# Token transposes of an attention group: four in one step, or spread over three, with the centring on another engine

## The chip, the cores and the metric

One Trainium2 chip, one of its cores. The metric is the device time of the whole program in microseconds (us); the kernel is launched once. TensorE multiplies matrices, VectorE, ScalarE and GpSimd work on tiles of 128 rows, and SyncE (SP) issues the DMAs. In the profile they are PE (with PEld for its weight loads), DVE, ACT, POOL and SP.

## The reference

`x` is 64 graphs of 128 tokens with 512 features, `adj` a 128 x 128 mask for each graph. Two passes of masked attention with 8 heads of 64 features run one after the other, then a feed-forward layer. What is computed, cut to what matters:

```python
def attention_side(source, query_source, mask):        # n2e, then e2n
    q, k, v = query_source @ wq.T + bq, source @ wk.T + bk, source @ wv.T + bv
    w = softmax(where(mask > 0, q_h @ k_h.T * 64 ** -0.5, -inf))   # 8 heads
    return concat(w @ v_h)
edges = ln(attention_side(x, x, adj.T) + x, norm1_g, norm1_b)
nodes = ln(x + attention_side(edges, x, adj), norm2_g, norm2_b)
out = ln(nodes + gelu(nodes @ w1.T + b1) @ w2.T + b2, norm3_g, norm3_b)
return layernorm(x + out)
```

`ln(y)` is `(y - mean) / sqrt(var + eps) * g + b` over the 512 features of a token. The change lies between the mean and variance of the first two of these norms and the transposed result that the next pass reads.

## The kernel before, in words

The 8192 tokens are worked off in 16 groups of 4 graphs (512 tokens), once for each attention pass, so there are 32 attention groups g = 0 to 31 (0 to 15 the first pass, 16 to 31 the second), and then 16 groups of the feed-forward pass. Every fp32 operand of a projection is split in a high and a low part, and three matmuls make one product.

**A group is four steps**, u = 0 to 3, one for each pair of heads. On TensorE a step is: keys of the pair (12 matmuls of 128 x 512), queries (12), `weigh` (the probabilities of an earlier step times the values, 40 small matmuls into `att_out`), values of one graph (12), then `scores` of this step (12 matmuls of 128 x 256). `weigh` lags two steps: step u of group g weighs pair u - 2, and steps 0 and 1 weigh pairs 2 and 3 of the group before. So the tokens of group g - 1 are complete only in step 1 of group g. Values run ahead by two steps too: steps 0 and 1 make the values of graphs 2 and 3 of the group, steps 2 and 3 those of graphs 0 and 1 of the next.

**The other engines in a step.** VectorE: for the scores of the step before, mask and maximum (8 instructions, `mask_and_maximum`, L763), `value_rest` (L739), the low part of the probabilities (L772), the low parts of keys and queries (L744, L747, L752), and then `add_weighed` (L688 to L710), which adds the residual and takes the statistics; in step 1 it ends with the group's mean and variance (`att_moments`). ScalarE: 8 exponentials (L525), the high parts of probabilities, keys and queries, then splits of the source or of the queries, and the value's high part (L508). GpSimd: `value_low` (L631, L633) for each graph, the low part of the source, and the bias of the residual (`add_bias`, L651).

**The norm of group g - 1** runs beside group g. GpSimd's `inverse_spread` stands behind `value_low` of graph 3, which is in step 2: it waits for the moments, then makes var + eps (L614), minus the mean (L615), the inverse square root as a power (`att_rstd`, L617) and the product `att_offset` (L620). ScalarE's `centre` (L486) then applies scale and offset to the four graphs, in step 2 behind the queries' high part. The result stands in `att_even_sum` or, in odd groups, in `normed`. In step 3 come the **token transposes**: `turn` (L838) puts one graph's 128 x 512 as four 128 x 128 blocks through TensorE into the one bank `att_turn`, and ScalarE's `copy_turned` (L478, four instructions) applies gain and shift on the way to one of the two buffers of `turned`, from which SyncE's `store_turned` writes to DRAM. There is one bank, so a `turn` waits until the copy before it is done:

```python
turn 0; keys; turn 1; queries; weigh; turn 2; values; turn 3; scores     # step 3 on TensorE
```

**The order of the work** is written out by hand for each engine; there is no scheduler. Semaphores count upward (`centred`, `turned_ready`, `turned_copied`). SyncE's queue is in order as well: a `store_turned` that waits for its copy holds the loads and probability transposes behind it. The groups of a pass run as two written out, six rounds of a loop of two groups, and two written out (`over_groups`), so each engine jumps back five times in a pass; a group that begins behind such a jump is called a jump group here, the other groups plain.

## Time and profile before

| | |
|---|---|
| median of 3 runs | 3041.64 us (3040.52 to 3041.72) |
| the profiled execution, its own time | 3036.6 us |
| its span, first to last instruction | 3034.8 us |
| busy: PE, DVE, ACT, POOL | 2895.0, 1618.3, 1633.8, 1297.0 us |
| mean granted TensorE clock | 0.992 |

The page shows TensorE busy in nine tenths of nearly every slice. The two attention passes take about the first 1573 us, the feed-forward pass the rest. Busy time of TensorE says little alone, since its matmuls overlap each other; its idle time is read from the waits and from the timeline, which name what ended each wait.

### The profile page before, as it was taken

Reading aid. Unit: us, or ns where it says so; the run is one execution under the profiler, and the core shown is the slowest. Engines: PE = TensorE matmul, PEld = TensorE weight load, DVE = VectorE, ACT = ScalarE, POOL = GpSimd, SP = SyncE. Lnnn points to the kernel's source line nnn. Section 1 sums busy time; section 2 is a strip of 40 time slices with the busy share of each in tenths; the row PEclk is TensorE's granted clock in tenths of the full one; section 3 lists DMA queues with packets and bytes.
Section 4 is the critical chain, followed back from the end, with each engine's and each line's share of the span. In section 5 each row is a group of like instructions: output and inputs, shape, how many; then the busy total and the mean of one; then the engine's idle time right before and its main releaser. Section 6 shows DMA issues by size and latency. Waiting matters only on the chain.

```text
span 3034.8 us, 55254 instructions
## 1 busy us (share of the span) xinstructions
PE 2895.0 (95%) x17920; PEld 2397.2 (79%) x17920; DVE 1618.3 (53%) x5786; ACT 1633.8 (54%) x4266; POOL 1297.0 (43%) x1291
## 2 busy tenths in 40 slices
PE   8999999999899999999989999999999999999996
PEld 7888878788787777787867888888888888888885
DVE  7776877777776767676763323232332323233234
ACT  6778777778788887888874222222222222222221
POOL 3443534344355555555431443444344344434434
PEclk9999999999999999999999999999999999999998
DMA  6554544454566565656563011111011111100101
GB/s 192 119 117 119 116 113 111 110 124 118 131 161 157 149 163 143 167 142 163 139 171 118 29 56 49 56 55 55 28 35 55 48 55 55 55 28 34 56 35 63
DMA packets 488660, 295.40 MB, mean 97 GB/s; under 512 B 279585, under 2 KB 410785, under 8 KB 488481
## 3 DMA queue, kind: packets, MB, share of 16 engines
q1 hardware_dynamic: 488480, 293.49, 36.2%
q8 instruction: 53, 0.87, 0.1%
q14 instruction: 127, 1.03, 0.1%
HBM read 159.21 MB, written 67.11 MB: 75 GB/s over the span
## 4 chain that ended last, share of the span: by engine, by line
PE 58%; issue 21%; POOL 14%; ACT 3%; DVE 2%; DMA 1%; POOLq 0%; SPq 0%; ACTq 0%; DVEq 0%
PE proj L1336 23%; PE score L1350 12%; PE proj L1350 11%; PE proj L872 9%; POOL att_tokens L651 4%; POOL att_v L633 3%; POOL source_lo L646 3%; PE score L919 2%; POOL att_v L631 2%; POOL att_query_lo L640 1%; PE att_out L856 1%; ACT att_probs L525 1%; ACT turned L478 1%; POOL pool_scratch L101 1%; POOL att_rstd L617 1%
## 5 line engine op out<-in xcount | busy, mean ns | idle before, releaser
L1122 ACT ACTIVATE hidden<-proj,ffn_bias 128x512 f32<-128x512 f32 x256 | 176.4, 689 | 1016.5 <-PE proj L1336 1016.5
L1282 DVE TENSOR_TENSOR hidden_lo<-hidden,hidden_hi 128x512 fp32r<-128x512 f32 x256 | 203.6, 795 | 966.2 <-ACT hidden_hi L1115 966.2
L525 ACT ACTIVATE att_probs<-att_probs,att_minus_max 128x128 f32<-128x128 f32 x1024 | 397.2, 395 | 115.5 <-DVE att_minus_max L763 115.5
L101 POOL TENSOR_TENSOR pool_scratch<-pool_scratch 128x1 f32<-128x1 f32 x144 | 41.4, 288 | 731.2 <-DVE ffn_moments L1226 415.2
L772 DVE TENSOR_TENSOR att_p_lo<-att_probs,att_p_hi 128x512 f16<-128x512 f32 x256 | 188.5, 776 | 292.0 <-ACT att_p_hi L532 292.0
L763 DVE CUSTOM_DVE_ANT_0 att_probs<-score,att_mask 128x128 f32<-128x128 f32 x1024 | 226.3, 285 | 29.2 <-issue 15.6
L646 POOL TENSOR_TENSOR source_lo<-source_raw,source_hi 128x512 fp32r<-128x512 f32 x128 | 163.0, 1295 | 152.0 <-ACT source_hi L548 152.0
L478 ACT ACTIVATE turned<-att_turn,att_shift,att_gain 128x128 f32<-128x128 f32 x512 | 193.2, 459 | 63.6 <-PE att_turn L838 62.2
L872 PE MATMUL proj<-weight_v_hi,source_hi 128*128 128x512 f32 x512 | 211.9, 414 | 13.6 <-DVE weight_v_lo L722 11.1
L872 PE MATMUL proj<-source_hi,weight_k_hi 128*128 128x512 f32 x512 | 203.4, 397 | 3.7 <-DVE weight_k_lo L722 3.7
L1336 PE MATMUL proj<-source_hi,w_hi 128*128 128x512 f32 x512 | 201.7, 394 | 0.0
L1336 PE MATMUL proj<-source_lo,w_hi 128*128 128x512 f32 x512 | 201.7, 394 | 0.0
L1336 PE MATMUL proj<-source_hi,w_lo 128*128 128x512 f32 x512 | 201.7, 394 | 0.0
L872 PE MATMUL proj<-weight_v_hi,source_lo 128*128 128x512 f32 x512 | 201.6, 394 | 0.0
L525 ACT ACTIVATION_READ_ACCUMULATOR att_probs<-att_probs,att_minus_max 128x1 f32 x1024 | 197.6, 193 | 6.4 <-issue 6.4
L872 PE MATMUL proj<-source_hi,weight_k_lo 128*128 128x512 f32 x512 | 201.1, 393 | 0.0
L872 PE MATMUL proj<-source_lo,weight_k_hi 128*128 128x512 f32 x512 | 200.8, 392 | 0.0
L872 PE MATMUL proj<-weight_v_lo,source_hi 128*128 128x512 f32 x512 | 200.7, 392 | 0.0
L856 PEld LDWEIGHTS att_out<-att_v,att_pt_hi 128*128 128x128 f16 x3072 | 149.1, 98 | 37.8 <-issue 37.8
L1213 POOL TENSOR_TENSOR normed<-normed,gain_row 128x512 f32<-128x512 f32 x64 | 83.9, 1311 | 211.6 <-DMA normed<-nodes 211.6
L651 POOL TENSOR_TENSOR att_tokens<-att_tokens,bias_row 128x512 f32<-128x512 f32 x128 | 167.9, 1312 | 1.7 <-DMA att_tokens<-in_x 1.7
L919 PE MATMUL score<-att_k_hi,att_q_hi 128*128 128x256 f32 x512 | 148.6, 290 | 18.9 <-DVE att_q_lo L752 18.9
(159 smaller groups left out, 8550.3 us busy)
## 6 DMA issues: line engine op xcount, KB each, us to landing
att_tokens<-in_x SPq DMA_DIRECT2D x128, 256.0 KB, 3.0
source_raw<-in_x_t SPq DMA_DIRECT2D x16, 1024.0 KB, 5.7
edges_t<-turned SPq DMA_DIRECT2D x64, 256.0 KB, 2.5
source_raw<-edges_t SPq DMA_DIRECT2D x16, 1024.0 KB, 5.8
att_query_raw<-in_x_t SPq DMA_DIRECT2D x16, 1024.0 KB, 6.6
nodes_t<-turned SPq DMA_DIRECT2D x64, 256.0 KB, 2.6
source_raw<-nodes_t SPq DMA_DIRECT2D x16, 1024.0 KB, 7.9
normed<-nodes SPq DMA_DIRECT2D x16, 1024.0 KB, 5.7
```

The costliest lines, as they stand in the source:

```text
L478: last = nc.scalar.activation(turned[:, b % 2, c, :], turn_bank[:, c * P:(c + 1) * P], ACT.Identity, bias=shift_column[own][:, c:c + 1], s ...
L525: nc.scalar.activation(probs[:, j, :], probs[:, j, :], ACT.Exp, bias=minus_max[:, j:j + 1], scale=-1.0, accum_out=row_sum[:, side, j:j + 1 ...
L646: nc.gpsimd.tensor_tensor(source_lo[1 - parity][:, c, :], source_raw[:, c, :], source_hi[1 - parity][:, c, :].bitcast(F32), ALU.subtract). ...
L651: nc.gpsimd.tensor_tensor(pair(tokens, u), pair(tokens, u), bias_v[:, u * P:(u + 1) * P].rearrange("p (o d) -> p o d", o=1).to_broadcast([ ...
L763: nc.vector.tensor_tensor_reduce(out=probs[:, 4 * h + j, :], in0=score_bank[h][:, j * P:(j + 1) * P], in1=mask[:, 2 * h + j // 2, :], scal ...
L772: nc.vector.tensor_tensor(p_lo[:, 4 * h:4 * h + 4, :], probs[:, 4 * h:4 * h + 4, :], p_hi[:, 4 * h:4 * h + 4, :], ALU.subtract).then_inc(p ...
L856: last = nc.tensor.matmul(out, p, value, start=(i == 0), stop=(i == len(products) - 1))
L872: last = nc.tensor.matmul(bank[:], stationary, moving, start=(c == 0 and i == 0), stop=(c == C - 1 and i == 2))
L919: last = nc.tensor.matmul(score_bank[h][:, 2 * i * P:2 * (i + 1) * P].rearrange("p (s j) -> p s j", s=2), q, k, start=(n == 0), stop=(n == 2))
L1282: nc.vector.tensor_tensor(hidden_lo[:, c % 2, :], hidden[:, c % 2, :], hidden_hi[:, c % 2, :].bitcast(F32), ALU.subtract).then_inc(hidden_ ...
L1336: last = nc.tensor.matmul(up_bank[c % 2][:], w, s, start=(i == 0), stop=(i == len(products) - 1))
L1350: last = nc.tensor.matmul(down_bank[b][:], h, w, start=(c == 0 and i == 0), stop=(c == FC - 1 and i == 2))
```

## The change

Three things move; nothing is computed differently but for the form of the centring.

1. **TensorE.** For a group's norm, `turn` 0 now stands in step 2 of the next group, between queries and `weigh`; `turn` 1 in the same step in the middle of the values (`midway`); `turn` 2 in step 3 behind `weigh`; and `turn` 3 in step 0 of the group after that, behind `weigh`. In the last group (g = 31) turns 1 and 3 stand before the scores of steps 2 and 3.
2. **ScalarE** copies 0 and 1 at the end of step 2, copy 2 in step 3, copy 3 in step 0, and centres no more. **SyncE** stores graph 0 one place earlier and graph 3 behind a probability transpose in the next group's step 0.
3. **GpSimd** drops minus the mean and the offset, and centres itself right behind the inverse square root: four instructions `(y - mean) * rstd` on 128 x 512, then the queries' low parts and `add_bias` as before.

The diff, without the declarations:

```diff
@@ SyncE, the body of a group
             load_tokens(sp, g, own, 1)
-            if not below(g, 2):
-                store_turned(sp, g - 2, own, GB - 1)
...
             if not starts(g):
                 turn_probabilities(sp, C * g - 1)
+            if not below(g, 2):
+                store_turned(sp, g - 2, own, 3)
...
             turn_probabilities(sp, C * g + 1)
+            if not starts(g):
+                store_turned(sp, g - 1, before, 0)
...
             if not starts(g):
-                store_turned(sp, g - 1, before, 0)
                 store_turned(sp, g - 1, before, 1)
@@ ScalarE
-    def centre(act, g, parity, b):
-        if b == 0:
-            act.wait_ge(offset_ready, g + 1)
-        data = total[parity][:, b, :]
-        nc.scalar.activation(data, data, ACT.Identity, bias=offset[:, b:b + 1], scale=rstd[:, b:b + 1]).then_inc(centred, 1)
...
-                turning = u == C - 1 and not starts(g)
-                if turning:
-                    copy_turned(act, g - 1, before, 0)
...
                 key_high(g, own, u)
-                if turning:
-                    copy_turned(act, g - 1, before, 1)
                 query_high(g, own, u)
                 if u < 2:
                     split_source(g, parity, range(2 * u, 2 * u + 2))
+                if u == 0 and not below(g, 2):
+                    copy_turned(act, g - 2, own, 3)
                 if u == 2 and not starts(g):
-                    for b in range(GB):
-                        centre(act, g - 1, 1 - parity, b)
-                if turning:
+                    copy_turned(act, g - 1, before, 0)
+                    copy_turned(act, g - 1, before, 1)
+                if u == 3:
                     if own == 1 and after == 1:
                         split_queries(g + 1)
-                    copy_turned(act, g - 1, before, 2)
-                    copy_turned(act, g - 1, before, 3)
+                    if not starts(g):
+                        copy_turned(act, g - 1, before, 2)
+                    if at(g, last_group - 1):
+                        copy_turned(act, g - 1, before, 3)
@@ GpSimd
         nc.gpsimd.tensor_scalar(spread[:], moments[:, :, 1], EPS, None, ALU.add).then_inc(spread_ready, 1)
-        nc.gpsimd.tensor_scalar(minus_mean[:], moments[:, :, 0], -1.0, None, ALU.mult).then_inc(negated, 1)
         pool.wait_ge(spread_ready, g + 1)
         nc.gpsimd.tensor_tensor(rstd[:], spread[:], half[:], ALU.pow).then_inc(rstd_ready, 1)
-        pool.wait_ge(negated, g + 1)
-        pool.wait_ge(rstd_ready, g + 1)
-        nc.gpsimd.tensor_tensor(offset[:], minus_mean[:], rstd[:], ALU.mult).then_inc(offset_ready, 1)
+
+    def centre(pool, g, parity):
+        pool_gate(pool, rstd_ready, g + 1, pool_scratch)
+        for b in range(GB):
+            data = total[parity][:, b, :]
+            nc.gpsimd.tensor_scalar(data, data, moments[:, b, 0:1], rstd[:, b:b + 1], ALU.subtract, ALU.mult).then_inc(centred, 1)
...
             if not starts(g):
                 inverse_spread(pool, g - 1)
+                centre(pool, g - 1, 1 - parity)
@@ TensorE
+                if midway is not None and c == 1:
+                    turn(pe, *midway)
...
             for u in range(C):
-                turning = u == C - 1 and not starts(g)
-                if turning:
+                keys(g, parity, own, u)
+                queries(g, parity, own, u)
+                if u == 2 and not starts(g):
                     turn(pe, g - 1, 1 - parity, 0)
-                keys(g, parity, own, u)
-                if turning:
-                    turn(pe, g - 1, 1 - parity, 1)
-                queries(g, parity, own, u)
                 if u >= 2:
                     weigh(pe, g, parity, u - 2)
                 elif not starts(g):
                     weigh(pe, g - 1, 1 - parity, u + 2)
-                if turning:
+                if u == 0 and not below(g, 2):
+                    turn(pe, g - 2, parity, 3)
+                if u == 3 and not starts(g):
                     turn(pe, g - 1, 1 - parity, 2)
                 if u < 2:
                     values(g, parity, own, u + 2)
                 elif not at(g, last_group - 1):
-                    values(g + 1, 1 - parity, after, u - 2)
-                if turning:
-                    turn(pe, g - 1, 1 - parity, 3)
+                    values(g + 1, 1 - parity, after, u - 2, (g - 1, 1 - parity, 1) if u == 2 and not starts(g) else None)
+                if at(g, last_group - 1):
+                    if u == 2:
+                        turn(pe, g - 1, 1 - parity, 1)
+                    if u == 3:
+                        turn(pe, g - 1, 1 - parity, 3)
```

How instructions stand now. GpSimd before, in the second group of the loop, from `value_low` of graph 3 to the next bias (`pool_scratch` rows are one-column instructions that carry a wait inside the loop):

```order
L631 CAST att_v_1<-att_v_rest 128x512
L632 REGISTER_ALU
L633 TENSOR_TENSOR att_v_1<-att_v_rest,att_v_1 128x512 [waits att_v_middle_ready]
L101 TENSOR_TENSOR pool_scratch<-pool_scratch 128x1 [waits att_moments_ready]
L614 TENSOR_SCALAR att_spread<-att_moments 128x4
L615 TENSOR_SCALAR att_minus_mean<-att_moments 128x4
L617 TENSOR_TENSOR att_rstd<-att_spread,minus_half 128x4 [waits att_spread_ready]
L620 TENSOR_TENSOR att_offset<-att_minus_mean,att_rstd 128x4 [waits att_rstd_ready,att_negated]
L651 TENSOR_TENSOR att_tokens<-att_tokens,bias_row 128x4x128 [waits att_tokens_in3]
```

The same place of the changed kernel (its lines are numbered a few lower):

```order
L628 CAST att_v_1<-att_v_rest 128x512
L629 REGISTER_ALU
L630 TENSOR_TENSOR att_v_1<-att_v_rest,att_v_1 128x512 [waits att_v_middle_ready]
L101 TENSOR_TENSOR pool_scratch<-pool_scratch 128x1 [waits att_moments_ready]
L609 TENSOR_SCALAR att_spread<-att_moments 128x4
L611 TENSOR_TENSOR att_rstd<-att_spread,minus_half 128x4 [waits att_spread_ready]
L101 TENSOR_TENSOR pool_scratch<-pool_scratch 128x1 [waits att_rstd_ready]
L617 TENSOR_SCALAR att_even_sum<-att_even_sum,att_moments,att_rstd 128x512 x4
L648 TENSOR_TENSOR att_tokens<-att_tokens,bias_row 128x4x128 [waits att_tokens_in3]
```

The four centring instructions stand between the inverse square root and the bias, still behind `value_low` of graph 3. TensorE, the same loop, step 2 of the changed kernel, from the last query matmul to the scores (before, the row of `att_out` with its waits followed the queries directly, and no transposes stood in this step):

```order
L836 MATMUL att_turn<-att_identity,normed 128x128 [waits att_turned_copied,att_centred]
L836 MATMUL att_turn<-att_identity,normed 128x128 x3
L843 ISA
L845 ISA [waits att_summed,att_values_ready]
...
L877 ISA
...
L836 MATMUL att_turn<-att_identity,normed 128x128 [waits att_turned_copied,att_centred]
L836 MATMUL att_turn<-att_identity,normed 128x128 x3
```

The first transposes of a group now ask for the centring ahead of `weigh` of step 2, and the second stand between the two halves of the values.

## Rows read from the trace of the kernel before

**Rows 1.** The page, groups of instructions: busy us, mean ns | idle before, releaser.

```profile
L478 ACT ACTIVATE turned<-att_turn,att_shift,att_gain 128x128 f32<-128x128 f32 x512 | 193.2, 459 | 63.6 <-PE att_turn L838 62.2
```

**Rows 2.** Waits of TensorE over the whole span: waited for, us in total, times, longest.

```profile
PE att_turn L838 <- ACT turned L478: 62.2, 47, 3.4
```

**Rows 3.** Windows of four groups, from keys of step 0 to the next: length, busy (instructions), clock, DMA.

```profile
392.70:441.99 49.29, 46.03 (x371) 38.72 (x370) 37.05 (x163) 37.64 (x113) 20.62 (x25) 1.00 0.48 113
441.99:489.18 47.19, 45.62 (x370) 38.73 (x369) 34.63 (x152) 37.50 (x113) 20.38 (x25) 1.00 0.49 117
1129.47:1177.64 48.17, 45.91 (x371) 38.68 (x370) 34.81 (x152) 39.47 (x117) 26.38 (x30) 1.00 0.61 158
1177.64:1228.51 50.87, 46.28 (x370) 38.60 (x369) 35.91 (x163) 39.60 (x117) 25.47 (x30) 1.00 0.59 150
```

**Rows 4.** Timeline of TensorE, first pass: start us, us, engine, line, [idle before, releaser].

```profile
416.22 0.40 PE L872 MATMUL proj<-source_hi,weight_k_hi 128*128 128x512 f32 x1
...
422.14 0.25 PE L856 MATMUL att_out<-att_v,att_pt_hi 128*128 128x64 bf16 x3 [0.29 <-POOL att_v L633]
...
427.58 0.60 PE L838 MATMUL att_turn<-att_identity,normed 128*128 128x128 f32 x4
...
427.94 0.48 PE L872 MATMUL proj<-source_hi,weight_k_hi 128*128 128x512 f32 x1
...
463.84 0.40 PE L872 MATMUL proj<-source_hi,weight_k_hi 128*128 128x512 f32 x1
...
474.77 0.60 PE L838 MATMUL att_turn<-att_identity,att_even_sum 128*128 128x128 f32 x4
```

**Rows 5.** Timeline of VectorE, first pass: the first mask-and-maximum of a step.

```profile
394.74 0.29 DVE L763 CUSTOM_DVE_ANT_0 att_probs<-score,att_mask 128x128 f32<-128x128 f32 x1
...
406.30 0.28 DVE L763 CUSTOM_DVE_ANT_0 att_probs<-score,att_mask 128x128 f32<-128x128 f32 x1
...
417.45 0.28 DVE L763 CUSTOM_DVE_ANT_0 att_probs<-score,att_mask 128x128 f32<-128x128 f32 x1
...
441.46 0.29 DVE L763 CUSTOM_DVE_ANT_0 att_probs<-score,att_mask 128x128 f32<-128x128 f32 x1 [0.68 <-issue]
...
463.67 0.29 DVE L763 CUSTOM_DVE_ANT_0 att_probs<-score,att_mask 128x128 f32<-128x128 f32 x1
```

**Rows 6.** Timeline of GpSimd, step 2 of one group of the first pass.

```profile
420.05 0.61 POOL L631 CAST att_v<-att_v_rest 128x512 bf16<-128x512 f32 x1
...
420.74 1.17 POOL L633 TENSOR_TENSOR att_v<-att_v_rest,att_v 128x512 bf16<-128x512 f32 x1
...
422.57 0.57 POOL L614 TENSOR_SCALAR att_spread<-att_moments 128x4 f32<-128x4 f32 x1
...
423.42 1.04 POOL L617 TENSOR_TENSOR att_rstd<-att_spread,minus_half 128x4 f32<-128x4 f32 x1
...
424.60 0.20 POOL L620 TENSOR_TENSOR att_offset<-att_minus_mean,att_rstd 128x4 f32<-128x4 f32 x1
...
424.75 1.29 POOL L651 TENSOR_TENSOR att_tokens<-att_tokens,bias_row 128x512 f32<-128x512 f32 x1
```

**Rows 7.** Timeline of ScalarE in the same step: the centring.

```profile
424.83 2.93 ACT L486 ACTIVATE normed<-normed,att_offset,att_rstd 128x512 f32<-128x512 f32 x4 [0.82 <-POOL att_offset L620]
```

**Rows 8.** Timeline of VectorE, second pass: the first mask-and-maximum of steps 0 and 2.

```profile
1178.72 0.29 DVE L763 CUSTOM_DVE_ANT_0 att_probs<-score,att_mask 128x128 f32<-128x128 f32 x1
...
1203.15 0.28 DVE L763 CUSTOM_DVE_ANT_0 att_probs<-score,att_mask 128x128 f32<-128x128 f32 x1
```

**Rows 9.** Timeline of ScalarE, second pass, behind the loop's jump: a gap between exponentials.

```profile
1184.30 0.20 ACT L525 ACTIVATION_READ_ACCUMULATOR att_probs<-att_probs,att_minus_max 128x1 f32 x1 [1.37 <-issue]
```

**Rows 10.** Timeline of TensorE: the third transposes of group 31.

```profile
1565.97 0.63 PE L838 MATMUL att_turn<-att_identity,att_even_sum 128*128 128x128 f32 x4 [3.45 <-ACT turned L478]
```

**Rows 11.** Timeline of TensorE: the keys behind its longest wait between the passes.

```profile
782.58 0.79 PE L872 MATMUL proj<-source_hi,weight_k_hi 128*128 128x512 f32 x1 [3.69 <-DVE weight_k_lo L722]
```

**Rows 12.** Windows: those twelve key matmuls, columns as in rows 3.

```profile
782.58:787.03 4.45, 4.45 (x12) 3.23 (x12) 3.71 (x7) 3.05 (x7) 0.00 (x0) 0.65 0.00 2
```

18 lines of the change are left out of this document (7 added, 11 removed).

## The prediction

> **What bounds the kernel now.** I read the page first, where TensorE is busy nearly throughout and ScalarE's copies idle mostly for TensorE [rows 1], then TensorE's waits, then windows and timelines of single groups. Of TensorE's waits the largest in the attention passes is the one that the change aims at: transposes wait 62.2 us in 47 places for the copy that empties their bank [rows 2]. The windows [rows 3] show what a group takes, from the keys of step 0 to those of the next group: in the first pass 49.29 us behind the loop's jump and 47.19 in a plain group, in the second 50.87 and 48.17. Nothing is slowed there by TensorE's clock, granted in full in all four. A step without transposes takes TensorE 10.93 us (463.84 to 474.77, rows 4), a block of four transposes 0.36 us (427.58 to 427.94, rows 4). Four steps and four blocks are 45.2 us, so 2 to 5.7 us of a group are waits.
>
> TensorE is not alone at the limit. VectorE's step, from one first mask-and-maximum to the next, takes 11.15 us in step 1 (406.30 to 417.45, rows 5), more than TensorE's 10.93. What stands in step 2 behind VectorE and GpSimd is therefore late by nature: GpSimd's cast of the values starts only at 420.05 [rows 6], and `weigh`, with everything else done, waits 0.29 us for GpSimd at 422.14 [rows 4]. The new place of the first transposes is in front of that `weigh`, and they wait for more of GpSimd than it does.
>
> **The change, part by part.** *Removed.* The 62.2 us of waits for the copy [rows 2] go. The copies have time now: between blocks 0 and 1 TensorE does `weigh` and half the values, some 2.6 us, and a copy takes 1.5 (193.2 us over 128 copies, rows 1) and two hand-overs; the other gaps are whole steps. ScalarE loses 2.93 us of centring in each group [rows 7]. I cost that at nothing: it lay beside TensorE's values and scores.
>
> *The new wait: when the first transposes can start.* I count from M, the first mask-and-maximum of step 2 (417.45, rows 5). From there GpSimd gets the last value, and its chain is shown [rows 6]. The variance instruction ends at 423.14; with a hand-over of 0.14 (424.46 to 424.60) the power starts at 423.28, 0.14 earlier than now, since minus the mean is gone, and ends at 424.32. The one-column instruction with its wait and the hand-over behind it are 0.14 each, so centring starts at 424.60. Then one centring, then 0.23 to reach TensorE (421.91, the end of the value's subtraction, to `weigh` at 422.14).
>
> No row shows a GpSimd instruction with two scalars per row on 128 x 512. The nearest below is the cast of one tensor, 0.61 us, the nearest above the addition of two tensors, 1.29 us [rows 6]. It reads one tensor, so I stay by the cast and take 0.70 for the second operation. The transposes then start at 425.53, that is M + 8.08.
>
> The Trainium skill (GPSIMD Engine Reference, Elementwise — side-by-side cycle accounting) gives 2.6 cycles an element for two inputs and 769 ns as the measured best case for 512 elements of a tight loop; by that the sum would be 2 us higher. The same page (Engine selection) speaks against moving elementwise work to GpSimd at all; here it is not the duration but the place in the chain that costs.
>
> *What follows them.* Block 0.36, `weigh` to the end of scores 5.44 (422.14 to 427.58, rows 4), block 1 0.36, then step 3 with block 2, 11.29: together 17.45 us to the next group's keys.
>
> *Plain group.* Counted from its keys at 441.99 [rows 3]: the first mask stands at -0.53 (441.46, rows 5), bound by the scores. Step 0 carries block 3 now, 11.29, so the next mask is at 10.76; 11.15 later, at 21.91, comes M. Transposes at 29.99, next keys at 47.44. TensorE would have been there after 11.29 + 10.93 + 5.6 (keys and queries, 416.22 to the end before 422.14), at 27.8: it waits 2.2 us. Against 47.19 that is +0.25 in the first pass, against 48.17 it is -0.73 in the second [rows 3].
>
> *Jump group.* VectorE's first mask comes 2.04 late (394.74 against 392.70), M 22.71 behind it [rows 5]: transposes at 32.83, TensorE there at 29.1, a wait of 3.7 us; the group takes 50.28 against 49.29, +0.99. In the second pass M comes 24.43 behind the first mask [rows 8], 1.37 of it a gap in ScalarE's exponentials that waits for nothing shown [rows 9]. If the gap stays, 52.00 against 50.87, +1.1; if it goes (ScalarE jumps earlier now), -0.2. I take the middle, +0.45.
>
> *Sum.* Nine plain and five jump groups in each pass: 9 x 0.25 + 5 x 0.99 - 9 x 0.73 + 5 x 0.45 = +2.9. At the ends of the passes, group 31 waits 3.45 us for a copy [rows 10] and group 15 the average of 1.3 (62.2 over 47); about 1 us is left where two blocks stand around one `weigh`: -4. Without the clock: -1.1.
>
> *The clock.* Behind an idle time of 3.69 us [rows 11] twelve key matmuls took 4.45 us at a mean granted clock of 0.65 [rows 12], that is for a part at 1.2 GHz instead of 2.4, where twelve otherwise take 2.8: 1.65 lost. The four windows, with waits of 1.3 us on average, hold the full clock [rows 2, 3]; in the ten jump groups there would be one of 3.7 us each. I take four falls, +6.6; the bounds are none, 0, and all ten, +16.5.
>
> The Trainium skill (TensorE: Matmul & The Clock Gate, HAM oscillation) warns of just this pattern, a wait in every round that lets the clock fall in every round. By it the sum would take all ten, 10 us more.
>
> Edits with one answer: the stores move behind copies that move too. The store of graph 0 stands in front of a token load that must wait for step 2's sums anyway, the store of graph 3 in front of one that waits for step 0's; the next use of each buffer is a step away. GpSimd's four centrings, 2.8 us, delay only the bias behind them, 1.29 us [rows 6], whose sums are read a step later, and the next value; GpSimd is busy 21 to 26 us of a group [rows 3], so there is room. In the feed-forward pass they stand alone.
>
> So +5.5 on the profiled execution's own 3036.6 us: 3042.1. The median of the three runs lies 5.0 above that execution: **3047 us**.
>
> **The rivals.**
>
> *A slow centring on GpSimd (slower).* At 1.29 us, like the addition, every group's transposes wait 0.59 more: 31 x 0.59 = 18.3, and waits of 4.3 us in jump groups let the clock fall in eight, +6.6: 3072. Each tenth costs 3.1 us; from 0.75 on the result is more than 0.2% above. For it: two operations and two scalars. Against it: the cast's time.
>
> *The clock holds and the gap goes (faster).* Centring at 0.61 (-2.8), no fall (-6.6), ScalarE's gap gone (-3.4): 3034. For it: ScalarE is two microseconds freer at the jump, and the waits of now cost no clock in the windows. Against it: 3.69 us did.
>
> *The wait is simply gone (faster).* If the first transposes didn't wait at their new place, all 62.2 us would go: 2979. It needs a chain 3.7 us shorter in the jump groups and 2.2 in the plain ones; nothing in rows 6 leaves that, but a place where the order differs from what I see can't be excluded.
>
> *SyncE's queue (slower).* A store that waits for its copy holds the transposes of probabilities behind it. At 1 us a group: 3078. It decides only if a copy comes over 4 us later than I have it.
>
> **How the numbers follow.** A measurement of this kernel tells about 0.2%, 6 us, from no change. Forecast 0.46: its own bounds (centring 0.61 to 0.85, clock falls 0 to 10) run from 3038 to 3061, so faster 0.04, within 0.22, slower 0.20. Slow centring 0.20, all slower. Clock and gap 0.24: 0.18 faster, 0.06 within. Wait gone 0.04. Queue 0.06. Faster 0.26, within 0.28, slower 0.46. The range 3026 to 3074 leaves out the wait that is gone, the queue and the tails.
>
> **What would show it.** In TensorE's waits the row of transposes waiting for the copy nearly vanishes, and one of transposes waiting for GpSimd's centring takes its place, with 70 to 80 us, 2.2 in plain groups and 3.7 in jump groups. The centring's mean time is 0.7. The second pass's plain groups take 47.4 us. The granted clock drops in some jump groups of step 2. I am wrong if the first transposes start well before M + 8, if the waits are gone without a new one, or if plain groups of both passes fall below 46.5.

## The result, and the profile after

The changed kernel takes 3089.99 us (median of 4 runs, 3087.70 to 3092.62), the kernel before on the same chip 3041.08 us (4 runs). The ratio is 1.0162, with a 95% interval of 1.0144 to 1.0180: slower by 1.6%, outside the noise. The profiled execution has a span of 3090.8 us against 3034.8, +56.0, and that difference is what the following takes apart.

The page of the change, TensorE's busy time first, then the group that answers to [rows 1] (columns as there):

```profile
PE 2909.6 (94%) x17920; PEld 2437.4 (79%) x17920; DVE 1658.5 (54%) x5786; ACT 1548.6 (50%) x4138; POOL 1564.1 (51%) x1379
...
L480 ACT ACTIVATE turned<-att_turn,att_shift,att_gain 128x128 f32<-128x128 f32 x512 | 192.5, 457 | 205.9 <-PE att_turn L836 205.8
```

The copies take as long as before, and idle three times as long for the transposes, which costs nothing: they have time now. TensorE's waits, the view of [rows 2]:

```profile
PE att_turn L836 <- POOL normed L617: 63.9, 15, 4.8
...
PE att_turn L836 <- POOL att_even_sum L617: 52.5, 16, 3.7
...
PE score L919 <- DVE att_q_lo L750: 10.1, 11, 1.5
...
PE att_turn L836 <- ACT turned L480: 2.6, 2, 2.1
```

The wait for the copy has gone from 62.2 to 2.6 us, as meant. In its place stand 116.4 us of waits for GpSimd's centring, one in each of 31 groups: 4.8 us in the jump groups, 2.6 to 3.8 in the others. (The third row, the waits of the scores for VectorE's low part of the queries, was 18.9 us before.) Where the waits for the centring come from shows on GpSimd in step 2 of a group behind the loop's jump, the stretch that answers to [rows 6]:

```profile
447.45 0.61 POOL L628 CAST att_v<-att_v_rest 128x512 bf16<-128x512 f32 x1
...
448.14 1.17 POOL L630 TENSOR_TENSOR att_v<-att_v_rest,att_v 128x512 bf16<-128x512 f32 x1
...
449.88 0.67 POOL L609 TENSOR_SCALAR att_spread<-att_moments 128x4 f32<-128x4 f32 x1
...
450.64 1.03 POOL L611 TENSOR_TENSOR att_rstd<-att_spread,minus_half 128x4 f32<-128x4 f32 x1
...
451.93 4.14 POOL L617 TENSOR_SCALAR normed<-normed,att_moments,att_rstd 128x512 f32<-128x512 f32 x2
```

The last row is two of the four centrings, 4.14 us, so 2.07 each; the means over the span are 2.09 and 2.13. The chain up to it is as in [rows 6]. TensorE gets its first block in a plain group and in this one at:

```profile
402.05 0.66 PE L836 MATMUL att_turn<-att_identity,att_even_sum 128*128 128x128 f32 x4 [3.29 <-POOL att_even_sum L617]
...
454.06 1.12 PE L836 MATMUL att_turn<-att_identity,normed 128*128 128x128 f32 x4 [4.82 <-POOL normed L617]
```

The second of these rows has more to tell than its 4.82 us of wait. Its four transposes take 1.12 us instead of 0.66. From the transposes to the end of the scores the same 72 matmuls ran in both groups. Their windows, columns as in [rows 3], and behind them the window of the attention passes as a whole:

```profile
402.05:408.43 6.38, 6.38 (x72) 5.80 (x73) 3.01 (x18) 3.66 (x10) 6.38 (x4) 1.00 0.50 102
...
454.06:462.53 8.47, 8.46 (x72) 7.67 (x73) 3.10 (x18) 3.66 (x10) 7.38 (x4) 0.73 0.48 96
...
50.00:1690.00 1640.00, 1497.88 (x11644) 1268.15 (x11643) 1181.83 (x4883) 1143.46 (x3475) 975.61 (x890) 0.96 0.52 129
```

Behind the wait of 3.29 us the clock was at 1.00, behind that of 4.82 us at 0.73 on average, that is for about half of the stretch at 1.2 GHz instead of 2.4, and the stretch took 2.1 us more. Over the attention passes the mean clock is 0.96. Before it was 0.99:

```profile
50.00:1610.00 1560.00, 1458.67 (x11635) 1227.30 (x11635) 1138.35 (x4877) 1225.43 (x3597) 714.22 (x805) 0.99 0.55 135
```

In the trace's record of the granted clock the change has 27 stretches at half clock before the span's last one, 133 us in all; such a stretch is called a fall here. They follow the first transposes in all ten jump groups and in 13 of the other 21, and four stand at the ends of the passes. The kernel before has 3, 24 us, all at the ends of the passes. What a fall costs can be read from plain groups of the change that differ in nothing else, from the keys of step 0 to the next: without a fall, with one of 3.4 us, with one of 6.8 us:

```profile
370.89:419.74 48.85, 45.56 (x370) 38.74 (x369) 36.87 (x156) 34.96 (x108) 28.92 (x28) 1.00 0.46 113
...
473.84:524.25 50.41, 47.12 (x370) 39.93 (x369) 36.84 (x154) 34.97 (x108) 28.92 (x28) 0.97 0.45 110
...
578.91:630.29 51.38, 48.09 (x371) 40.94 (x370) 36.81 (x154) 34.97 (x108) 28.92 (x28) 0.93 0.44 108
```

That is 1.6 us for the shorter and 2.5 us for the longer.

**A part that the change does not touch became faster.** I divide the span at one instruction that is the same in both, the first matmul of the feed-forward pass with weights in a tile named `w..._hi`. It stands before and after at

```profile
1617.03 0.39 PE L1350 MATMUL score<-w_hi,hidden_hi 128*128 128x512 f32 x1
```

```profile
1695.63 0.39 PE L1346 MATMUL score<-w_hi,hidden_hi 128*128 128x512 f32 x1
```

So the part up to it grew by 78.6 us, and the rest, 1417.8 us before, is 1395.2 us, 22.6 less. The two parts are called attention and feed-forward below, though the first holds some 44 us of the feed-forward pass's beginning as well. In the same 300 us of full clock and full load TensorE ran 1304 matmuls before and 1325 after (windows of before, then of after):

```profile
2000.00:2300.00 300.00, 300.00 (x1304) 244.22 (x1303) 91.23 (x178) 78.75 (x123) 123.51 (x104) 1.00 0.16 54
```

```profile
2000.00:2300.00 300.00, 300.00 (x1325) 248.43 (x1324) 90.53 (x175) 78.36 (x122) 118.83 (x98) 1.00 0.16 54
```

### The profile page after: what moved, and what is told of

It is laid out like the page before. It is cut to its first block, busy times and chain, and to the rows that moved or that the text cites. A ratio compares the mean times of both kernels' runs of the same rounds, so it can differ in the third digit from the quotient of the medians.

```text
span 3090.8 us, 55194 instructions
## 1 busy us (share of the span) xinstructions
PE 2909.6 (94%) x17920; PEld 2437.4 (79%) x17920; DVE 1658.5 (54%) x5786; ACT 1548.6 (50%) x4138; POOL 1564.1 (51%) x1379
## 3 DMA queue, kind: packets, MB, share of 16 engines
q1 hardware_dynamic: 488480, 293.49, 35.5%
## 4 chain that ended last, share of the span: by engine, by line
PE 53%; POOL 23%; issue 18%; DVE 3%; ACT 1%; DMA 1%; POOLq 0%; SPq 0%; DVEq 0%; ACTq 0%
PE proj L1332 22%; PE score L1346 11%; PE proj L1346 11%; PE proj L870 6%; POOL att_tokens L648 4%; POOL normed L617 3%; POOL att_even_sum L617 3%; POOL source_lo L643 3%; POOL att_v L630 3%; POOL att_v L628 2%; POOL att_query_lo L637 1%; POOL pool_scratch L101 1%; PE att_out L854 1%; POOL att_rstd L611 1%; PE score L919 1%
## 5 line engine op out<-in xcount | busy, mean ns | idle before, releaser
L101 POOL TENSOR_TENSOR pool_scratch<-pool_scratch 128x1 f32<-128x1 f32 x168 | 47.7, 284 | 673.5 <-DVE ffn_moments L1222 402.8
L770 DVE TENSOR_TENSOR att_p_lo<-att_probs,att_p_hi 128x512 f16<-128x512 f32 x256 | 223.4, 911 | 207.2 <-ACT att_p_hi L528 207.2
L870 PE MATMUL proj<-weight_v_hi,source_hi 128*128 128x512 f32 x512 | 225.2, 440 | 11.4 <-DVE weight_v_lo L720 11.4
L870 PE MATMUL proj<-weight_v_lo,source_hi 128*128 128x512 f32 x512 | 208.6, 407 | 0.0
L870 PE MATMUL proj<-weight_v_hi,source_lo 128*128 128x512 f32 x512 | 207.9, 406 | 0.0
L854 PEld LDWEIGHTS att_out<-att_v,att_pt_hi 128*128 128x128 f16 x3072 | 165.6, 103 | 26.9 <-issue 25.7
L854 PE MATMUL att_out<-att_v,att_pt_hi 128*128 128x64 bf16 x3072 | 181.5, 200 | 0.0
L648 POOL TENSOR_TENSOR att_tokens<-att_tokens,bias_row 128x512 f32<-128x512 f32 x128 | 178.3, 1393 | 1.6 <-DMA att_tokens<-in_x 1.6
```

What stands on the lines that cost most here:

```text
L648: nc.gpsimd.tensor_tensor(pair(tokens, u), pair(tokens, u), bias_v[:, u * P:(u + 1) * P].rearrange("p (o d) -> p o d", o=1).to_broadcast([ ...
L770: nc.vector.tensor_tensor(p_lo[:, 4 * h:4 * h + 4, :], probs[:, 4 * h:4 * h + 4, :], p_hi[:, 4 * h:4 * h + 4, :], ALU.subtract).then_inc(p ...
L854: last = nc.tensor.matmul(out, p, value, start=(i == 0), stop=(i == len(products) - 1))
L870: last = nc.tensor.matmul(bank[:], stationary, moving, start=(c == 0 and i == 0), stop=(c == C - 1 and i == 2))
```

## The experiments

Theory A: the loss is the length of one centring, since it stands in the chain from step 2's masks to the first transposes. Rivals: B, GpSimd's added load slows VectorE and GpSimd's own duties; C, the spreading itself, with the stores elsewhere in SyncE's queue. Later came L, that tile addresses made the feed-forward pass faster, and the question of what the clock costs by itself. All runs in one table; "attention" and "feed-forward" are the two parts of the profiled span divided as above, "waits" those of TensorE's transposes for a centring or a copy, "falls" the stretches at half clock and their length, without the span's last one. Each ratio is to the kernel before as measured beside that run (medians 3038.2 to 3041.9 us).

| kernel | waits us | falls (us) | attention us | feed-forward us | median us | ratio to before, 95% |
|---|---|---|---|---|---|---|
| before | 62.2 | 3 (24) | 1617.0 | 1417.8 | 3041.1 | |
| the change | 119.0 | 27 (133) | 1695.6 | 1395.2 | 3090.0 | 1.0144 to 1.0180 |
| spread only, ScalarE centres | 98.7 | 18 (96) | 1668.3 | 1417.6 | 3091.9 | 1.0155 to 1.0189 |
| GpSimd centring only | 60.8 | 5 (21) | 1608.9 | 1395.1 | 3006.3 | 0.9873 to 0.9906 |
| short centring | 79.6 | 17 (75) | 1636.8 | 1395.3 | 3032.9 | 0.9966 to 0.9985 |
| first centring early | 5.4 | 4 (27) | 1560.8 | 1394.9 | 2956.9 | 0.9709 to 0.9742 |
| change at old addresses | 116.3 | 28 (137) | 1696.9 | 1418.1 | 3112.9 | 1.0214 to 1.0248 |
| before at new addresses | 61.1 | 7 (24) | 1617.8 | 1395.1 | 3013.7 | 0.9891 to 0.9924 |
| first centring on VectorE | 8.4 | 3 (24) | 1541.2 | 1395.2 | 2936.5 | 0.9639 to 0.9671 |
| idle time filled | 15.7 | 2 (10) | 1652.6 | 1399.5 | 3054.8 | 1.0036 to 1.0069 |

### The spread alone, centring on ScalarE

```diff
+                    for b in range(GB):
+                        centre(act, g - 1, 1 - parity, b)
                     copy_turned(act, g - 1, before, 0)
...
-                centre(pool, g - 1, 1 - parity)
```

with `minus_mean`, `offset` and their two instructions on GpSimd back as before.

> The spread of the transposes alone: PE, SyncE and the copies as in the change, the centring back on ScalarE, in step 2 behind the query conversion and ahead of copies 0 and 1. Theory A (the loss is the length of one centring, 2.07 us on GpSimd, which stands in the chain from step 2's masks to the first transpose): ScalarE's centring takes 0.73 us, so the first transposes start 1.3 to 1.4 us earlier, PE's waits for them fall from 116 us to about 70 (2.1 in a plain group, 3.6 in a group whose step 1 jumps), and the time is 3040 to 3055 us. Theory B (GpSimd's extra 268 us of work slows VectorE and GpSimd's own duties, wherever the transposes stand): also faster than the change, but VectorE's conversions of the probabilities back at 0.74 us and PE's waits for transposes about as long as in the change. Theory C (the spreading itself, with the stores in other places of SyncE's queue, costs the time): 3080 us or more.

TensorE's waits:

```profile
PE att_turn L841 <- ACT normed L478: 51.1, 15, 4.0
...
PE att_turn L841 <- ACT att_even_sum L478: 39.9, 16, 2.7
...
PE att_turn L841 <- ACT turned L486: 7.7, 17, 1.7
```

The waits for the centring fell by 25 us to 91.0. A had said about 70; by its own 2.1 and 3.6 us a group that should have read 88. The second block now waits too, 0.3 us in 15 of 17 places, for the first copy, which ScalarE does behind four centrings. But the time did not fall at all: 3091.9 us, where A expected 3055 at most and C 3080 or more. Yet the attention passes did get shorter, 1668.3 against 1695.6 us, which C does not explain; this run alone doesn't settle it. The rest of the answer is in the column beside it: the feed-forward pass is back at 1417.6. That gave theory L.

### GpSimd's centring alone

```diff
                 inverse_spread(pool, g - 1)
+                centre(pool, g - 1, 1 - parity)
```

in the kernel before, with ScalarE's centring taken out; the transposes stay together in step 3.

> The other half alone: the kernel before, all four transposes in step 3 as there, with nothing changed but that GpSimd centres right behind the inverse square root. Theory A: the first centring ends some 5 us or more before the first transposes of step 3, so its 2.07 us cost nothing and PE's waits for transposes stay with ScalarE's copies (62 us before); ScalarE has 2.9 us a group less to do; 3025 to 3045 us. Theory B (GpSimd's load and what it takes from VectorE): 3065 us or more, with PE waiting for biases, values or keys and not for transposes.

TensorE's wait for the copy, and GpSimd's centring in one group (two of the four):

```profile
PE att_turn L834 <- ACT turned L478: 60.8, 47, 3.1
```

```profile
425.91 4.15 POOL L615 TENSOR_SCALAR normed<-normed,att_moments,att_rstd 128x512 f32<-128x512 f32 x2
```

The same 2.07 us (4.15 for two) cost nothing where the transposes come a step later: 1608.9 us for the attention passes, 8 fewer than before. Theory B falls: GpSimd does the same 268 us of centring here and TensorE waits for none of it. The time is 3006.3 us, faster than A's 3025 to 3045, since the feed-forward pass is again the fast one; this kernel too has no `minus_mean` and `offset`.

### A short centring

```diff
-            data = total[parity][:, b, :]
+            data = total[parity][:, b, 0:P]
```

> The change with its centring instruction cut to the first 128 of 512 columns; the rest of the centring is left out, all else stays, transposes included. Theory A: one centring falls from 2.07 to about 0.6 us, the first transposes start 1.45 us earlier, PE's waits for them go from 3.3 to 1.8 us in a plain group and from 4.8 to 3.4 in the others, and with 31 groups and fewer clock falls the time is 3030 to 3050 us. Theory C (spreading and SyncE's order): over 3075 us.

The centring (view of groups: busy us, mean ns), then TensorE's waits:

```profile
L617 POOL TENSOR_SCALAR att_even_sum<-att_even_sum,att_moments,att_rstd 128x128 f32<-128x128 f32 x64 | 55.0, 874 | 0.4
```

```profile
PE att_turn L836 <- POOL normed L617: 44.1, 15, 3.6
...
PE att_turn L836 <- POOL att_even_sum L617: 32.0, 16, 2.4
```

This kernel leaves out three quarters of the centring. The centring went from 2.1 to 0.8 or 0.9 us (A had said 0.6) and the waits for it from 116.4 to 76.1 us: 40.3 us for 31 groups, 1.3 us each, so the first transposes follow the centring's length one to one. A holds, and some 2.0 to 2.4 us in most plain and 3.5 in jump groups remain, which lie in the chain ahead of it. The clock fell behind all ten waits of 3.5 us, and in 4 of the 21 groups with 1.3 to 2.4.

### The first centring early

```diff
+                inverse_spread(pool, g - 1)
+                centre(pool, g - 1, 1 - parity, range(1))
             value_low(g, parity, 3)
...
-                inverse_spread(pool, g - 1)
-                centre(pool, g - 1, 1 - parity)
+                centre(pool, g - 1, 1 - parity, range(1, GB))
```

> The change with its whole work, but on GpSimd the inverse square root and the first centring go ahead of the fourth value's two instructions, since the moments are ready about 0.3 us after step 2's masks begin; centrings 2 to 4 stay behind the value. Theory A (PE waits only for the end of this chain): the first centring ends 4.3 us after the moments, 1.5 us before PE comes to the transposes, so nearly all of the 116 us of waits goes; the fourth value is up to 1 us late for the products (0 to 30 us in all); 2965 to 3010 us, with few clock falls. Theory B or C: 3050 us or more, since GpSimd's load, SyncE's order and the places of the transposes are those of the change.

GpSimd in step 2 of a jump group, where centring now precedes the value:

```profile
411.52 1.04 POOL L611 TENSOR_TENSOR att_rstd<-att_spread,minus_half 128x4 f32<-128x4 f32 x1
...
412.81 2.09 POOL L618 TENSOR_SCALAR normed<-normed,att_moments,att_rstd 128x512 f32<-128x512 f32 x1
...
415.00 0.61 POOL L629 CAST att_v<-att_v_rest 128x512 bf16<-128x512 f32 x1
...
415.70 1.48 POOL L631 TENSOR_TENSOR att_v<-att_v_rest,att_v 128x512 bf16<-128x512 f32 x1
```

TensorE in the same group, then its waits over the span:

```profile
415.14 0.60 PE L839 MATMUL att_turn<-att_identity,normed 128*128 128x128 f32 x4
...
417.42 0.25 PE L857 MATMUL att_out<-att_v,att_pt_hi 128*128 128x64 bf16 x3 [1.68 <-POOL att_v L631]
```

```profile
PE att_out L857 <- POOL att_v L631: 22.5, 25, 1.7
...
PE att_turn L839 <- ACT turned L480: 5.4, 2, 3.7
```

The first transposes start at 415.14, behind the centring that ends at 414.90, and wait for nothing; the longest wait in these rows is now the 1.68 us that `weigh` waits for the value. The waits for a centring are gone from the list, the falls of the clock are 4, all at the ends of the passes, and the kernel takes 2956.9 us, 2.7% less than the kernel before and 8 us below the range given under A, which did not yet count the faster feed-forward pass. It does everything that the change does, with two calls in another order. This rules out B and C: GpSimd's load, SyncE's order and the places of the transposes are those of the change. VectorE's conversion of the probabilities takes 776 ns on average before, 911 in the change and 1052 here, and the centring is not the cause: it takes 892 with the centring on ScalarE and 912 with the short one. The conversions above 0.9 us (17 of 256 before, 54 in the change, 49 with ScalarE's centring, 108 here) all begin while GpSimd runs a `TENSOR_TENSOR`, or the cast right ahead of one, while those that begin under a running centring take 0.68 us, as beside an idle GpSimd. That this slowing decides nothing is argued from TensorE's waits, not tried.

### Addresses

```diff
-            **NORM_TILES}.items()}
+            "pad0": [P, GB], "pad1": [P, GB], **NORM_TILES}.items()}
```

in the change; and in the kernel before the reverse, with its two small tiles laid into one that is free at the time:

```diff
+    minus_mean, offset = (m.feed_forward["stats"][:, i, 0:GB] for i in range(2))
```

> The change, with two unused tiles of 128x4 in the place where minus_mean and offset lay before, so that every tile behind them (the feed-forward pass's second to fourth weight blocks and its hidden tiles among them) lies at the addresses of the kernel before: 64 bytes higher per partition, 64 above a multiple of 128 bytes and not on one. The feed-forward pass, whose code the change does not touch beyond its start, took 1395.2 us in the change and 1417.8 in the kernel before, with 1325 and 1304 matmuls in the same 300 us. Theory L (the addresses do it): 1417 us for that pass and 3108 to 3118 us in all. Theory S (something else that the change does, such as the store order or the centring's engine, does it): 1395 us for that pass and 3086 to 3096 in all.

> The kernel before, with minus_mean and offset laid in the feed-forward pass's tile of statistics, which is free at that time, and nothing else changed: the tiles behind them lie at the addresses of the change. Theory L: feed-forward pass 1395 us, in all 3014 to 3020 us, so that the change's own loss against a kernel of the same addresses is some 73 us. Theory S: 1418 us and 3036 to 3044 us.

The window of the feed-forward pass, the change at the old addresses and then the kernel before at the new ones:

```profile
2000.00:2300.00 300.00, 300.00 (x1303) 244.22 (x1303) 89.72 (x171) 76.98 (x120) 123.36 (x102) 1.00 0.16 54
```

```profile
2000.00:2300.00 300.00, 300.00 (x1325) 248.48 (x1324) 90.14 (x174) 78.89 (x124) 125.75 (x105) 1.00 0.16 54
```

Both came out as theory L says, the second 0.3 us below its range: 1303 matmuls in 300 us with the pad, 1325 without the tiles; 1418.1 and 1395.1 us; and the attention passes hardly move (1.3 and 0.8 us). The removal of two tiles of 16 bytes a partition, each of which takes 32 in the allocation, is worth 23 to 28 us by itself. At equal addresses the change loses more than its own ratio shows: 3090.0 against 3013.7 us, 2.5%, or 3112.9 against 3041.9, 2.3%. The run with ScalarE's centring stands at the old addresses: against the change there it is 21.0 us faster, still less than the 35 to 50 that A had said.

### What makes the centring long

The four centrings of a group in four forms (the centring itself is left out):

```diff
+        nc.gpsimd.tensor_scalar(d0, d0, moments[:, 0, 0:1], None, ALU.subtract).then_inc(centred, 1)
+        nc.gpsimd.tensor_scalar(d1, d1, 0.5, 1.0, ALU.subtract, ALU.mult).then_inc(centred, 1)
+        nc.gpsimd.tensor_scalar(d2, d2, 0.5, None, ALU.subtract).then_inc(centred, 1)
+        nc.gpsimd.tensor_tensor(d3, d3, moments[:, 3, 0:1].to_broadcast([P, D]), ALU.subtract).then_inc(centred, 1)
```

> A measurement of GpSimd: the four centrings of a group in four forms of one 128x512 float32 instruction each, in the place of the centring (the centring itself is left out): subtract one per-partition scalar; subtract and multiply with two immediates; subtract one immediate; subtract a broadcast column as a tensor. The full form (two per-partition scalars) took 2.07 us. Theory A1 (every operation costs a pass of about 1 us over the elements): 1.0 to 1.3, 2.0, 1.0 to 1.3, 1.2 to 1.3 us. Theory A2 (the per-partition scalars make it slow): 1.5 to 2, 1.2, 1.2 and 1.2 us. Theory A3 (any tensor_scalar of this size is slow against a tensor_tensor): about 2 us for the first three and 1.2 for the last.

```profile
394.04 1.57 POOL L616 TENSOR_SCALAR att_even_sum<-att_even_sum,att_moments 128x512 f32<-128x512 f32 x1
...
395.70 1.93 POOL L617 TENSOR_SCALAR att_even_sum<-att_even_sum 128x512 f32<-128x512 f32 x1
...
397.59 1.49 POOL L618 TENSOR_SCALAR att_even_sum<-att_even_sum 128x512 f32<-128x512 f32 x1
...
399.05 1.04 POOL L619 TENSOR_TENSOR att_even_sum<-att_even_sum,att_moments 128x512 f32<-128x512 f32 x1
```

None of the three accounts is right alone. A `TENSOR_SCALAR` with one operation and one immediate takes 1.49 us, a per-partition scalar in its place adds 0.08 us, the second operation 0.44, and the same subtraction as a `TENSOR_TENSOR` with a broadcast column takes 1.04 (means of 32 each: 1.62, 1.93, 1.54, 1.05). So the kind of instruction carries most, the second operation the rest. Two tensor instructions would be an estimated 2.08 us, no better than the 2.07 of the centring. This kernel ran once, and no time is drawn from it.

### The first centring on VectorE

```diff
                     value_rest(g, parity, u + 1)
+                    if u == 2 and not starts(g):
+                        gate(dve, rstd_ready, g, dve_scratch[:, 2 + GB:3 + GB])
+                        centre_first(nc.vector, g - 1, 1 - parity)
```

with a semaphore of its own, and on GpSimd the inverse square root ahead of the fourth value and centrings 2 to 4 behind it.

> The change with the inverse square root ahead of the fourth value on GpSimd, as in the run with the early first centring, but the first centring on VectorE, in its idle 1.75 us between the masks of step 2 and the conversion of the probabilities; GpSimd does the fourth value next and then centrings 2 to 4. Theory A: the fourth value is no longer late, so the 22.5 us of waits of the products for it go, the first transposes still find their block centred, and the time falls by 10 to 25 us from 2957 to 2932 to 2947 us. If VectorE's 0.7 to 0.8 us push the conversion of the probabilities and with it the second step's chain back: 2957 to 2985 us.

VectorE in step 2, then TensorE's wait for the transposes:

```profile
408.96 0.09 DVE L768 DVE_READ_ACCUMULATOR2_ANT att_minus_max<- 128x1 f32 x1
...
409.57 0.55 DVE L616 TENSOR_SCALAR normed<-normed,att_moments,att_rstd 128x512 f32<-128x512 f32 x1
...
411.41 1.72 DVE L777 TENSOR_TENSOR att_p_lo<-att_probs,att_p_hi 128x512 f16<-128x512 f32 x2 [1.29 <-ACT att_p_hi L529]
```

```profile
PE att_turn L849 <- ACT turned L481: 8.4, 13, 3.8
```

The same instruction takes 0.55 us on VectorE against 2.07 on GpSimd, in a gap that was idle. Of the 8.4 us of waits for a copy 5.5 stand in two places at the end of the second pass. The value is no longer waited for, and the conversion behind it (411.41) still starts when ScalarE lets it, after 1.29 us of idle time. 2936.5 us: 20 us less than with the early centring, 3.4% less than the kernel before and 5.0% less than the change.

### The idle time filled

What the clock costs by itself:

```diff
+        if b == 0:
+            for _ in range(FILL):
+                nc.tensor.transpose(turn_bank[:, 0:P], identity[:], identity[:])
         pe.wait_ge(centred, GB * g + b + 1)
```

with FILL = 30, and the wait for the empty bank moved ahead of them.

> The change, with 30 more transposes of the identity into the turn bank (their result is overwritten) ahead of each group's first block, where TensorE stands idle for GpSimd's centring: at the full clock about 2.7 us (0.09 each, as in a block of four at 0.36), less than the waits of 3.3 and 4.8 us, so that by themselves they cost nothing. The change has 27 falls of the granted clock in the attention passes against 3 in the kernel before. If the idle time in front of the first transposes is what lets the clock fall and the falls carry a part of the loss worked out at about 36 us (the attention passes' 78.6 us less 43 us of added waits), then the waits shrink to 0.6 and 2.1 us, the falls to 10 or fewer, and the time is 3050 to 3070 us although every wait still ends when it did. If the falls cost nothing beside the waits, or come from something else (the spread transposes themselves), the time stays at 3085 to 3095 us or rises by what the added transposes cost.

TensorE's waits, and the attention passes' window (column PEclk):

```profile
PE proj L874 <- issue: 12.1, 10, 1.6
...
PE att_turn L840 <- POOL normed L618: 11.4, 11, 1.6
...
PE att_turn L840 <- POOL att_even_sum L618: 2.3, 6, 0.4
```

```profile
50.00:1650.00 1600.00, 1553.62 (x12588) 1333.72 (x12587) 1180.00 (x4889) 1147.86 (x3480) 979.43 (x891) 1.00 0.57 133
```

With more work on TensorE and the same chain in front of the transposes the kernel is 35 us faster than the change, and its attention passes are 43.1 us shorter: the clock is at 1.00 on average instead of 0.96, with 2 falls instead of 27. That is 1.7 us for each of 25, beside the 1.6 and 2.5 us read from single groups above. It is a net figure: the filled kernel also has ten waits of TensorE for its own instructions, 12.1 us (the first row), that the change does not have, and how much of them other waits cover is not shown. The feed-forward pass took 4.3 us more here; 3.3 of them are the last group's 30 added transposes, which stand in that pass (1668.88 to 1672.15) where TensorE would not have waited. For the remaining 1.0 us I have no cause.

## Why the prediction was wrong

It said 3047 us with a range to 3074; the kernel takes 3090. The direction was right, the size was not. Its sum was +5.5 us on the profiled execution and the outcome is +56. By its steps:

**"Removed" was right.** The wait for the copy went from 62.2 to 2.6 us. So was the kind of the new wait: in every group one, for the centring, and in jump groups longer than in plain ones, by 1.5 us in the first pass and 1.2 in the second.

**The centring was mis-sized, and so were its bounds.** The step that failed was "No row shows a GpSimd instruction with two scalars per row": between a cast of 0.61 and an addition of 1.29 us I took 0.70 and treated 1.29 as the upper end. It is 2.07. A `TENSOR_SCALAR` of this size with a single operation is at 1.5 already above that upper end, and the cast, the nearest below in elements, says nothing of it. The extra 1.37 us in 31 groups are 42.5 us; the short centring confirms the slope, 1.3 us of wait for 1.2 to 1.3 us of length. The rival "slow centring" had the mechanism and the slope, "each tenth costs 3.1 us", and stopped at 1.29; that slope carried on to 2.07 gives 3047.1 + 42.5 = 3089.6, and with the rival's own eight falls 3096. That the first is the measured time is chance: the clock's +36.5 stands against -22.6 and -5.9 of the terms below, and the rest is in how the profiled executions lie to their medians. The Trainium skill (GPSIMD Engine Reference, Elementwise — side-by-side cycle accounting) gives 769 ns as the measured best case for 512 elements and 2.6 cycles an element for two inputs, at the page's 1.2 GHz an estimate of 1.1 us. The trace disagrees with both for this instruction, 2.07; the two-input figure is given for `tensor_tensor`, and there 1.04 with the broadcast column agrees with the estimate.

**The clock was priced right and counted wrong.** I had 1.65 us a fall; it was 1.7. This is the second step that failed: I took four falls and bounded them by ten, one for each jump group; there were 24 more than before, and the filled kernel shows 43.1 us for 25 of them. I had argued from [rows 3] that waits of 1.3 us hold the clock, and from [rows 11, 12] that one of 3.69 us does not, and left plain groups out altogether. They had 2.6 to 3.8 us, and the clock fell in 13 of 21. With ScalarE's centring (1.8 to 3.3 us in these groups) it fell in 6 of 21, with the short centring (1.3 to 2.4) in 4 of 21, and in jump groups, with waits of 3.5 us and more, in all ten of each of these kernels. In the kernel before a group has one wait for a copy of 1.5 to 1.6 us, in the second pass another of 0.7, and the second pass's jump groups one of 1.7 to 2.6 us for the low part of the queries, which my average of 1.3 over the copy waits left out; there is no fall behind any of them. At the new addresses the same kernel has two such falls, behind waits of 2.7 and 2.6 us. Part of this follows from the first error, part would have been there without it: the short centring's attention passes are 19.8 us longer than before with 17 falls. The Trainium skill's warning of a wait in every round (TensorE: Matmul & The Clock Gate, HAM oscillation — how this bites in real kernels) is what these traces show, in 13 of the other 21 groups too.

**The geometry was right in plain groups and off in the second pass's jump groups.** A plain group of the first pass without a fall takes 48.85 us (the window above), where my 47.44 with the true centring is 48.81. Inside it two small misses cancel: from the mask M of step 2 to the transposes it is 9.20 us (to 454.06, from the row below), not 8.08 + 1.37 = 9.45, and from the transposes to the next keys 17.69 (402.05 to 419.74), not 17.45.

```profile
444.86 0.29 DVE L761 CUSTOM_DVE_ANT_0 att_probs<-score,att_mask 128x128 f32<-128x128 f32 x1
```

A plain and a jump group of the first pass are 97.7 us together by my count, and with the true centring 2.74 more, 100.5. In the filled kernel, where the clock holds, a pair takes 101.2 us (VectorE's mask instruction, which comes once a group; two groups lie between these rows), and in the change 106.2:

```profile
210.74 0.43 DVE L802 TENSOR_SCALAR att_mask<-att_adj 128x512 f32<-128x512 f32 x1
...
311.93 0.43 DVE L802 TENSOR_SCALAR att_mask<-att_adj 128x512 f32<-128x512 f32 x1
```

```profile
214.92 0.43 DVE L801 TENSOR_SCALAR att_mask<-att_adj 128x512 f32<-128x512 f32 x1
...
321.10 0.43 DVE L801 TENSOR_SCALAR att_mask<-att_adj 128x512 f32<-128x512 f32 x1
```

Over all groups the filled kernel's attention passes are 35.5 us longer than before; less 42.5 for the centring that is -7, where my sum without the clock had -1.1. Two things in the second pass's jump groups are larger than this difference of 5.9. I put the first mask 2.04 us behind the keys, a figure of the first pass; [rows 3] and [rows 8] have 1177.64 and 1178.72, 1.08 us. So the group comes to 51.04 and not 52.00, 4.8 us less over five groups. And ScalarE's gap, of which I counted half, went altogether: in the second pass its exponentials have 6.4 us of such gaps before and none in the change, 3.4 us less than I had. What stands against them by some 2 us I have not taken apart.

**A term was missing.** "Minus the mean is gone" was costed at 0.14 us in a chain. That its tile was gone too was never costed, and it gave 22.6 us in a pass that I had called untouched. No row of the kernel before could show that; that a removed tile moves the tiles behind it could be read from the declarations, not what that does to the time.

Together: +5.5 forecast, +42.5 for the centring, +36.5 for the clock (43.1 instead of 6.6), -5.9 for the geometry, -22.6 for the addresses: +56.0. The geometry's term is what the others leave of the measured +56.0, so that the sum fits is no check of it. The rival with SyncE's queue played no part: stores and loads stand in the early-centring kernel as in the change, and it is the second fastest of all. "The wait is simply gone" was given 2979 us, and needed a chain shorter by 2.2 and 3.7 us; with two calls moved it was there, and at the new addresses it came to 2957.

## What to carry over

An operation that goes into the chain in front of the bound engine is priced by a measurement of that very form on that very engine, or given bounds much wider than the nearest rows (2.07 here against rows of 0.61 and 1.29); and before it is put there, look for what stands ahead of it on its own queue without need (here one value's two instructions; moving them behind took 4.3% off the change). Count a wait of the matrix engine twice: for its length, and for the clock behind it, which fell behind every wait of 3.5 us or more in the jump groups, behind some of 1.3 to 3.8 us in the others, and never within a pass in the two kernels with an early first centring, whose groups wait 1.7 us at most. And when a change removes or adds a tile, compare a stage that it does not touch before crediting the difference to anything else.

## What the runs showed of the hardware

- Shifting all tiles behind a point by 64 bytes a partition changed the rate of a pass of 128x512 float32 matmuls at full clock: 1325 against 1304 in 300 us, mean distance 226 against 230 ns. By the addresses that the allocation gives, the weight blocks and hidden tiles behind that point start on a multiple of 128 bytes in the fast layout (135040 for the second block) and 64 above one in the slow (135104). In the slow layout the matmuls with the shifted weight blocks show 394 ns against 391 for those of the same line with weights in tiles that did not move, and 389 for both in the fast layout. On the other line of the pass those with unmoved weights and moved hidden tiles show 395 to 396 ns in the slow layout, so it is not the weights alone. Which operand does it, whether 128 bytes is the rule, and what a shift by another 64 bytes does was not tried.
- GpSimd, 128x512 float32: `TENSOR_SCALAR` 1.49 us with one immediate, 1.57 with one scalar per partition, 1.93 with two immediates, 2.07 with two scalars per partition; `TENSOR_TENSOR` with a broadcast column 1.04. A quarter of the columns with two scalars takes 0.81 to 0.87 us on average, so of the 2.07 an estimated 0.4 us do not go with the length. VectorE takes 0.55 for the full form; in the kernel before the same form stands on VectorE in the feed-forward pass, with a median of 0.54 us and single ones up to 1.52.
- VectorE's 128x512 `TENSOR_TENSOR` from float32 to float16 takes 0.68 us beside an idle GpSimd and beside its `TENSOR_SCALAR` centring (14 that begin under one, in four kernels). One that begins under a GpSimd `TENSOR_TENSOR` ends some 0.55 us behind that instruction's end, up to 1.78 us in all.
- Added transposes in otherwise idle time made the kernel faster: 960 more matmuls, 35 us less. A fall of 3.4 us at half clock cost 1.6 us in a group, one of 6.8 us 2.5.
